# Last attention layer: natural and transposed scores draw on three shared PSUM areas by table, and the orders of TensorE, ScalarE and VectorE around them are rewritten

## What is computed

```python
xn  = group_norm(x, 32 groups) * gn_w + gn_b
gfeat = mean(xn) @ gproj_w.T + gproj_b
q, k, v = split(qkv_w @ xn + qkv_b)            # 8 heads of 8 channels
k = k + 0.1 * gfeat
attn = softmax(q.T @ k / sqrt(8))              # 256 x 256 for each image and head
out  = proj_w @ (attn @ v) + proj_b + 0.1 * gfeat + x
```

## Time and profile before

| | us |
|---|---|
| median of 3 runs | 78.75 |
| lowest, highest of them | 78.66, 90.68 |
| the profiled execution | 79.57 |
| its span | 77.5 |
| mean granted TensorE clock | 1.000 |

### The profile page before, as it was taken

One profiled execution on the slowest core, in us unless ns is written; L12 is line 12 of the kernel. 1 busy time (PEld: TensorE's weight loads), 2 busy tenths in 40 slices (PEclk: granted clock), 3 DMA queues, 4 the chain that ended last, 5 costly groups with the idle time before them and its releaser, 6 DMA issues.

```text
span 77.5 us, 1620 instructions
## 1 busy us (share of the span) xinstructions
PE 69.7 (90%) x597; PEld 47.5 (61%) x597; DVE 52.6 (68%) x106; ACT 45.4 (59%) x103; POOL 13.5 (17%) x46
## 2 busy tenths in 40 slices
PE   3999989799779999999989999998999998999950
PEld 3869856666438746587567875775665866544300
DVE  1133954676675561977679997979879788997560
ACT  1531889528229933761443377888878986698100
POOL 7999000000000000011002860202020201200000
PEclk9999999999999999999999999999999999999999
DMA  0981000000000000000000000000000000000003
GB/s 18 266 314 66 0 0 0 0 8 0 0 0 4 0 0 8 0 0 0 4 0 0 0 0 0 0 8 0 0 0 0 0 8 0 0 0 8 0 30 106
DMA packets 1303, 1.65 MB, mean 21 GB/s; under 512 B 144, under 2 KB 912, under 8 KB 1296
## 3 DMA queue, kind: packets, MB, share of 16 engines
q1 hardware_dynamic: 1008, 1.41, 5.6%
q10 hardware_dynamic: 288, 0.14, 0.7%
HBM read 1.29 MB, written 0.26 MB: 20 GB/s over the span
## 4 chain that ended last, share of the span: by engine, by line
PE 67%; DVE 15%; ACT 12%; issue 3%; DVEq 0%
PE PS L570 9%; PE PS L549 9%; PE PS L424 9%; PE PS L452 5%; PE PS L397 5%; ACT E L775 5%; PE PS L333 5%; DVE NM L1044 5%; PE PS L439 5%; PE PS L516 4%; ACT E L823 4%; PE PS L499 3%; PE PS L354 3%; PE PS L380 2%; PE PS L529 2%
## 5 line engine op out<-in xcount | busy, mean ns | idle before, releaser
L1044 DVE TENSOR_REDUCE NM<-PS 128x4 f32<-128x1024 f32 x16 | 19.5, 1223 | 2.3 <-PE PS L516 2.0
L823 ACT ACTIVATE E<-PS 128x1024 f32<-128x1024 f32 x16 | 16.2, 1023 | 1.8 <-PE PS L549 1.4
L775 ACT ACTIVATE E<-PS,NM 128x256 f32<-128x256 f32 x24 | 11.0, 476 | 3.5 <-DVE NM L935 3.4
L935 DVE TENSOR_REDUCE NM<-PS 128x2 f32<-128x512 f32 x12 | 7.6, 685 | 4.9 <-PE PS L424 4.9
L570 PE MATMUL PS<-E,VA 128*32 128x256 f32 x128 | 8.8, 386 | 0.1
L816 ACT ACTIVATE QKS<-PS,W 128x512 fp32r<-128x512 f32 x8 | 5.5, 686 | 5.2 <-PE PS L499 5.1
L549 PE MATMUL PS<-QSA,QKS 32*128 32x256 f32 x64 | 8.0, 324 | 0.6 <-ACT E L823 0.2
L549 PEld LDWEIGHTS PS<-QSA,QKS 32*128 32x128 f32 x64 | 5.0, 183 | 5.0 <-issue 3.7
L333 PE MATMUL PS<-idle 128*128 128x256 f32 x31 | 6.7, 354 | 1.2 <-DVE idle L920 1.2
L516 PE MATMUL PS<-QKS 24*128 24x256 f32 x64 | 6.9, 298 | 0.6 <-ACT QKS L816 0.5
L284 POOL TENSOR_TENSOR GM<-GM,half_pow 128x1 f32<-128x1 f32 x2 | 1.1, 562 | 34.1 <-DVE GM L992 34.1
(11 more groups left out here) (125 smaller groups left out, 120.6 us busy)
## 6 DMA issues: line engine op xcount, KB each, us to landing
W<-pack SPq DMA_DIRECT2D x2, 256.0 KB, 4.4
W<-pack SPq DMA_DIRECT2D x1, 352.0 KB, 5.0
X<-x SPq DMA_DIRECT2D x2, 128.0 KB, 2.5
out<-Y SPq DMA_DIRECT2D x2, 128.0 KB, 1.7
W<-pack ACTq DMA_DIRECT2D x1, 72.0 KB, 2.7
W<-pack ACTq DMA_DIRECT2D x1, 64.0 KB, 2.7
```

The lines of the kernel that those rows point to most:

```text
L775: e = act.activation(E[p][b][:, half, :], bank[:, half * N:(half + 1) * N], ACT.Exp, bias=NM[p][b][:, half:half + 1], accum_out=SUM[p][:, ...
L823: act.activation(E3[u % 3][:, 2 * two:2 * two + 2, :, :].rearrange("k j m q -> k (j m q)"), t_of(u, two)[:, :], ACT.Exp, scale=float(HD) * ...
L935: dve.tensor_reduce(NM[p][b][:, :], bank.rearrange("r (h c) -> r h c", h=2), AX.X, ALU.max, negate=True).then_inc(maxima[p], 1)
L1044: dve.tensor_reduce(to, score_bank(two).rearrange("q (j h k) -> q j h k", j=2, h=2), AX.X, ALU.max, negate=True).then_inc(maxima3, 1)
```

## The change

Two tables name the area of every group of scores: `NATURAL[u][two]` and `TRANSPOSED[u][two]`, each with `low`, `mid` (the former `t_banks`) or `high`. Four more tables name the wait of each group: so many maxima or so many exponentials taken. The orders of TensorE, ScalarE and VectorE in the last layer are written anew to fit. Among other things one of the two blocks of four idle matmuls there is dropped, `stack(2)`, `stack(4)` and `stack(5)` stand earlier, both groups of a unit's maxima stand ahead of its `add_max_rows` for units 3, 4 and 6, natural scores run up to a whole unit further ahead of the transposed ones, `low_keys(1)` and `low_queries(1)` come before the maxima of unit 2, `mix3(1)` to `mix3(4)` stand later among the score groups, and `score_t(7, 0)` and `score_t(7, 1)` enclose the first half of `mix3(5)`. `max_rows(u)` waits now for `add_max_rows(u - 1)` as well. The second output bank is another one. The number of score groups, maxima, exponentials, stacks and mixes is the same.

```diff
+NATURAL = [("low", "high"), ("low", "mid"), ("low", "mid"), ("high", "low"),
+           ("low", "high"), ("mid", "low"), ("low", "mid"), ("low", "mid")]
+TRANSPOSED = [("high", "high"), ("low", "mid"), ("mid", "low"), ("high", "mid"),
+              ("high", "high"), ("high", "low"), ("high", "mid"), ("high", "mid")]
+NATURAL_AFTER_MAXIMA = {(1, 0): 1, (2, 0): 3, (2, 1): 4, (4, 0): 8, (4, 1): 7, (6, 0): 12,
+                        (7, 0): 13, (7, 1): 14}
+NATURAL_AFTER_EXPS = {(3, 0): 2, (3, 1): 3, (5, 0): 5, (5, 1): 6, (6, 1): 8}
+TRANSPOSED_AFTER_MAXIMA = {(0, 0): 2, (1, 0): 5, (1, 1): 6, (2, 1): 9, (3, 0): 10,
+                           (3, 1): 11, (5, 1): 15, (6, 1): 16}
+TRANSPOSED_AFTER_EXPS = {(0, 1): 1, (2, 0): 4, (4, 0): 7, (4, 1): 9, (5, 0): 10, (6, 0): 11,
+                         (7, 0): 13, (7, 1): 14}
...
-        out_banks = [stack_bank, bank_b[1]]
+        out_banks = [stack_bank, bank_c[1]]
...
             def t_of(u, two):
-            return t_late if two == 1 and u >= 6 else t_banks
+            return areas[TRANSPOSED[u][two]]
...
             def max_rows(u):
                 pe.wait_ge(max_parts, u + 1)
+                if u >= 1:
+                    pe.wait_ge(aug_out, u)
...
@@ mix3
                 elif u == 4:
-                    pe.wait_ge(maxima3, 2 * UNITS - 1)
+                    pe.wait_ge(exps3, 12)
```

More of the change, by code:

```diff
@@ L157, in conv_attention_chain @@
         s_low, s_high = PS[0][:, 0:1024], PS[1][:, 1024:2048]
-        t_banks, mix_bank, turn_bank = PS[1][:, 0:1024], bank_c[0], bank_a[0]
+        s_mid, mix_bank, turn_bank = PS[1][:, 0:1024], bank_c[0], bank_a[0]
+        areas = {"low": s_low, "mid": s_mid, "high": s_high}
         stack_bank = bank_d[0]
-        t_late = PS[1][:, 1024:2048]
         row_bank = mix_bank[:, N:2 * N]
@@ L223, in rows_of_maxima, with scores_of @@
             return AUGW[u % 2][:, :, :].rearrange("q h (j r) -> q h j r", r=QUAD)
+        def scores_of(u, two):
+            return areas[NATURAL[u][two]]
         def t_of(u, two):
-            return t_late if two == 1 and u >= 6 else t_banks
+            return areas[TRANSPOSED[u][two]]
         def mix_of(u):
@@ L233, in mix_of @@
             return (stack_bank if 1 <= u <= 3 else mix_bank)[:, 0:N]
-        def score_bank(two):
-            return (s_low, s_high)[two]
         block = ctx.enter_context(nc.Block())
@@ L506, in score3 @@
                 pe.wait_ge(stack_out, u + 1)
-                if u > 0:
-                    pe.wait_ge(maxima3, 2 * u - 1 + two)
-                elif two == 1:
+                if (u, two) == (0, 1):
                     pe.wait_ge(x_new[1], 3)
-                bank = score_bank(two)
+                elif (u, two) == (1, 1):
+                    pe.wait_ge(turned_out[1], 2)
+                    pe.wait_ge(turned_out1[1], 2)
+                elif (u, two) in NATURAL_AFTER_MAXIMA:
+                    pe.wait_ge(maxima3, NATURAL_AFTER_MAXIMA[u, two])
+                elif (u, two) in NATURAL_AFTER_EXPS:
+                    pe.wait_ge(exps3, NATURAL_AFTER_EXPS[u, two])
+                bank = scores_of(u, two)
                 for half in range(2):
@@ L535, in score_t @@
                 pe.wait_ge(aug_out, u + 1)
[L536 to L542, removed]
+                if (u, two) in TRANSPOSED_AFTER_MAXIMA:
+                    pe.wait_ge(maxima3, TRANSPOSED_AFTER_MAXIMA[u, two])
                 else:
-                    pe.wait_ge(exps3, 2 * u + two)
+                    pe.wait_ge(exps3, TRANSPOSED_AFTER_EXPS[u, two])
                 for m in range(2):
@@ L676, in _ @@
             keep_clock(4, bank_b[1])
+            stack(2)
             score3(1, 0)
-            stack(2)
-            keep_clock(4, bank_b[1])
             score3(1, 1)
+            stack(3)
             max_rows(0)
-            stack(3)
+            score3(2, 0)
             score_t(0, 0)
-            score3(2, 0)
             project3(1)
             project_second()
+            max_rows(1)
             score_t(0, 1)
-            max_rows(1)
             score3(2, 1)
+            score_t(1, 0)
             values(3, XN[1], 1)
-            score_t(1, 0)
             score3(3, 0)
+            stack(4)
+            score3(3, 1)
+            score_t(1, 1)
             mix3(0)
-            score_t(1, 1)
-            score3(3, 1)
+            stack(5)
             max_rows(2)
-            stack(4)
+            score3(4, 0)
+            score3(4, 1)
             score_t(2, 0)
-            score3(4, 0)
-            stack(5)
+            mix3(1)
             score_t(2, 1)
             max_rows(3)
-            score3(4, 1)
-            mix3(1)
-            score_t(3, 0)
             score3(5, 0)
             stack(6)
+            score_t(3, 0)
             max_rows(4)
+            score3(5, 1)
             score_t(3, 1)
-            score3(5, 1)
             mix3(2)
@@ L719, in _ @@
             stack(7)
+            score3(6, 1)
+            score_t(4, 1)
             max_rows(5)
-            score_t(4, 1)
-            score3(6, 1)
+            score3(7, 0)
             mix3(3)
             score_t(5, 0)
-            score3(7, 0)
+            max_rows(6)
+            score3(7, 1)
+            score_t(5, 1)
+            score_t(6, 0)
             turn3()
[L728 to L733, removed]
             score_t(6, 1)
             max_rows(7)
+            mix3(4)
+            score_t(7, 0)
             mix3(5, (0,))
-            score_t(7, 0)
+            score_t(7, 1)
             mix3(5, (1,))
-            score_t(7, 1)
             mix3(6)
@@ L884, in _ @@
             exps_t(0, 1)
+            exps_t(1, 0)
             values3(1)
-            exps_t(1, 0)
+            stack_copy(4)
+            exps_t(1, 1)
             o_copy(0)
-            exps_t(1, 1)
-            stack_copy(4)
+            stack_copy(5)
             exps_t(2, 0)
-            stack_copy(5)
+            o_copy(1)
             exps_t(2, 1)
-            o_copy(1)
+            stack_copy(6)
             exps_t(3, 0)
-            stack_copy(6)
             exps_t(3, 1)
@@ L1043, in maxima_of @@
                 to = NM3[u % 2][:, :, 2 * two:2 * two + 2].rearrange("q h j -> q j h")
-                dve.tensor_reduce(to, score_bank(two).rearrange("q (j h k) -> q j h k", j=2, h=2),
+                dve.tensor_reduce(to, scores_of(u, two).rearrange("q (j h k) -> q j h k", j=2, h=2),
                                   AX.X, ALU.max, negate=True).then_inc(maxima3, 1)
@@ L1168, in _ @@
             add_max_rows(1)
-            maxima_of(2, 1)
             low_keys(1)
             low_queries(1)
+            maxima_of(2, 1)
             maxima_of(3, 0)
+            maxima_of(3, 1)
             add_max_rows(2)
-            maxima_of(3, 1)
             maxima_of(4, 0)
+            maxima_of(4, 1)
             add_max_rows(3)
-            maxima_of(4, 1)
             maxima_of(5, 0)
@@ L1185, in _ @@
             maxima_of(6, 0)
+            maxima_of(6, 1)
             add_max_rows(5)
-            maxima_of(6, 1)
             maxima_of(7, 0)
@@ L1193, in _ @@
             divide3()
+            add_max_rows(7)
             turn_units()
-            add_max_rows(7)
             divide_units()
```

## The result

| | before | after |
|---|---|---|
| median of 14 runs each, us | 79.18 | 78.06 |
| ratio after to before | | 0.9876, 95% interval 0.9835 to 0.9916 |
| profiled execution, us | 79.57 | 78.37 |
| its span, us | 77.5 | 76.2 |
| start of the first maxima of unit 0 | 40.47 | 40.25 |

The kernel got 1.2% faster; 2.5% were forecast. In the last layer, from the first maxima to the last transpose, it takes 31.02 us instead of 32.09: 1.07 us less where 1.9 were forecast. The other 0.2 of the span lies before the first maxima, in layers that the change does not touch; that stretch took between 39.4 and 41.0 us in the traces of this study. Some executions of most of these kernels lose TensorE's full clock part of the way; the ratios leave them out, the medians in the table don't.

What follows compares the result with a forecast made beforehand. The prediction took the handing to and fro of a single transposed buffer, 3.42 us a unit, as the bound. 2.1 us from the exponentials less 0.2 at the mixes gave 1.9 off 78.75: 76.85, rounded 76.8; range 75.4 to 79.0.

Steps and rivals of the forecast that it cites:

- What bounds the old kernel: Steady units: one transposed buffer passed to and fro, 1.71 us twice, 3.42 a unit; engines alone need about 3.0.
- The mechanism: Last layer: exponential (2,0) 0.6 late, then two transposed areas pay; last exponential 2.1 earlier, 0.15 to 0.2 lost at mixes.
- the waits of M for its addition: Rows of maxima, seven units: the added wait is never last, costs nothing; up to 0.15 each, 1.0 if it decides.
- two releasers: Table of what frees each exponential in units 3 to 7, such as the addition of unit 5 for (5,0) at 62.95.
- The sign "ScalarE busy over 7 of 8 us between 56 and 64": Units in the 56 to 64 us window: one of the signs listed to show the forecast right.
- the term for TensorE's own groups: TensorE's queue, one unit: group durations read from starts in the earlier trace, about 3.0 us together.
- ScalarE did not become the bound: Rival, units 5 to 7: ScalarE binds sooner, waits at T50, T60 and T70 vanish, 75.5 us; chance 0.12.
- The half-way case: Whole kernel: half-way to the rival that waits only move (79.0), 77.4 to 78.4 us; chance 0.20.
- the forecast's own spread: Whole kernel: 76.1 to 77.4 us around the forecast median of 76.8; chance 0.45.
- The start: Unit 0 and 1: stack 3 moves about 0.8 earlier without the idle matmuls; first exponential stays at 45.6.
- the rival on the other side: At 43 to 45 us, idle block gone: clock falls to 1.2 GHz, 4 us more, 80.8; chance 0.06.
- The rule that I weighed against the trace: TensorE's pauses: cycling PSUM banks with brief idling can lose the clock repeatedly; by it the change would slow.

Runs made afterwards that it cites:

- the probe: Kernel before with the two matmuls of max_rows issued three times in units 3 to 6: ratio 1.0207 (1.0119 to 1.0296).
- less work for TensorE: Changed kernel with the low-part matmuls left out of the stacks of units 5 to 7: 0.9897; the changed kernel beside it 0.9896.
- both single parts: Kernel before with only the new area tables: 90.87 and 92.05 us; with only the new orders: 94.42 and 97.82 us.

## Why the prediction was half right

Times of the changed kernel are moved by 0.22 us here, the difference of the first maxima.

| exponential | forecast | measured | late |
|---|---|---|---|
| (2,0) | 53.7 | 53.66 + 0.22 | 0.2 |
| (3,0) | 57.0 | 57.13 + 0.22 | 0.35 |
| (4,0) | 59.3 | 59.45 + 0.22 | 0.37 |
| (5,0) | 62.95 | 63.40 + 0.22 | 0.67 |
| (7,0) | 67.25 | 67.95 + 0.22 | 0.92 |
| reader of mix 7 | 70.65 | 71.27 + 0.22 | 0.84 |

*What bounds the old kernel* was half right. The transposed area handed to and fro at 1.71 us is there, but TensorE was nearly as full: it needs about 3.2 of 3.42 us, as the probe shows, not 3.0. In the new order two units, T30 at 56.44 to T50 at 62.86, take 3.21 each.

*The mechanism* was right in order and sign: (2,0) later than before and (4,0) earlier, two stack copies ahead of (2,0), the waits of M for its addition never last, mix 7 held by TensorE at the end. It was wrong in two releasers. For (5,0) I named the addition of unit 5; in the trace of after that addition ends at 62.45, and T50 stands behind mix 3 until 62.86. And T41 comes 1.71 after T40, not less, because unit 4 has one area for both. The sign "ScalarE busy over 7 of 8 us between 56 and 64" failed too; the window after has 6.61, and TensorE 8.00:

```profile
56.00:64.00 8.00, 8.00 (x88) 5.50 (x87) 6.89 (x8) 6.61 (x10) 0.82 (x4) 1.00 0.01 2
```

*The step that failed* is the term for TensorE's own groups: "T 0.31, N 0.36, stack 0.57, M about 0.2, T 0.31, N 0.36 and the mix about 0.9 to 1.0". From T20 (53.11) to N60 (59.25) stand five T, two N, one stack, two M and two mixes. By those prices 1.55 + 0.72 + 0.57 + 0.40 + 1.90 = 5.14 us, measured 6.14. The missing 1.0: two M at 0.37, 0.34; the stack at 0.67, 0.10; the mixes at 1.00, 0.10; T20, T21 and T30 alone at 0.43, 0.36; N50 alone, 0.07; the rest 0.03. My schedule had some waits in this stretch that the real queue fills, so less than 1.0 of it came out as lateness: 0.4 us at exponential (4,0), 0.9 at (7,0) after further groups of the same kinds. For M I took 0.2 of the 0.47 between 61.28 and 61.75 in the earlier trace rows as work and the rest as a wait for the exponential. For an M behind a stack and ahead of a T that was nearly right: the probe leaves 0.26 (0.71 less 0.45). In the new order M stands behind a T and ahead of an N, and there it costs 0.37. So the prices were those of the old order's neighbours, and nearly every T and N there has the other beside it: the new order splits several such pairs.

*The other cases*: ScalarE did not become the bound, though with less work for TensorE it stands right behind. The half-way case, 77.4 to 78.4, had 0.20, and the measured 78.06 is in it and in the range; the forecast's own spread ended at 77.4. Its reason, that waits I took as covered come back, was not the one: TensorE's groups were longer.

*The start.* "The first exponential still hangs on the maxima of unit 0 and stays at 45.6" was right (5.12 us after the first maxima, before 5.16), but only since the idle block is gone; I had named no work that the block's place is needed for, and that was the stack.

*The clock*, the rival on the other side, did not decide the comparison, but it is real: it fell in the traces of both single parts, of the kernel before without its second idle block, and in one of two profiled executions of the changed kernel. The kernel before loses it too, and the 90.68 us in the table ahead of the prediction was such an execution. "Such pauses left the clock at 1.00", as I argued from the earlier trace rows, was therefore too weak an argument, and the 4 us that I put on a fall were too few: 88 to 91 us instead of 79 for the kernel before, 85.2 to 85.4 instead of 78 for the changed one beside it. The idle matmuls of the earlier trace rows also don't show what the lower level costs, for the granted clock of the first 8 us of that trace is 1.00; the runs at 0.50 do, with a mix at 1.86 us for 1.00. The rule that I weighed against the trace, in the Trainium skill (TensorE: Matmul & The Clock Gate, A second HAM failure mode: psum-queue depth-cycling), agrees with the two runs of one part alone in this: pauses between groups while PSUM areas are handed round, and then 0.50. It speaks of a clock that goes to and fro; here each trace shows one fall that lasts until the last mixes.

## What to carry to other kernels

Price a queue of small matmuls by the starts of neighbours, each pair of kinds by itself, and look for the place where a kind is followed by something that surely doesn't wait: a gap behind a group that always precedes a wait isn't all wait. Before saying that an engine has slack, put known work on it. When a buffer is the bound and TensorE needs 93 or 94% of the same period, freeing the buffer brings the other 6 or 7% at most (here 3.42 to 3.21 us a unit); what is left is a matter of which groups stand side by side. And before an idle block is called dropped work, ask what moves into its place.

## What the runs showed of the hardware

- Groups of 4 matmuls with 24 or 32 rows: on different row groups two neighbours run side by side (0.44 us for both before a mix, and eight in 0.52), on the same ones 0.34 for the first and 0.33 for the second, alone 0.43. The Trainium skill (TensorE: Matmul & The Clock Gate, Part 3: Packing small matmuls — row/col tiling, The mechanism) says that weights load beside running matmuls only for other row groups; these starts agree.
- Clock: the trace of the kernel before without its second idle block shows 1.00 up to about 44 us and then 0.50 to the end of the scores. Its windows:

```profile
40.00:44.00 4.00, 3.46 (x29) 2.68 (x25) 3.78 (x7) 1.37 (x2) 1.83 (x7) 0.98 0.00 0
44.00:48.00 4.00, 4.00 (x19) 3.37 (x19) 2.88 (x6) 1.71 (x2) 1.64 (x3) 0.50 0.00 0
```

The changed kernel is busy 3.58 us in the same window and kept 1.00 in its trace. The fall doesn't come in every execution of one kernel. Among the runs taken side by side, the mean granted clock was under 0.95 in 8 of 12 executions of the kernel before without the block and in 9 of 29 with it, and in 5 of 8 of the changed kernel and in 1 of 12 with the block put back. That points to the block keeping the clock up in some executions; with so few it is not shown.
